# First layer's bias written into PSUM by ScalarE, PSUM's bits set by four early products of zeros, row sums moved to the second step

## The reference

```python
x = ln(x + L0(x, adj));  x = ln(x + L1(x, adj));  x = ln(x + L2(x, adj));  x = ln(x + L3(x, adj))

# L0
y = (adj @ x + x) @ weight + bias
y = y / max(sqrt(sum(y * y, axis=2)), 1e-12)
# L1: five steps of a gated update
m = adj @ h;  av = concat([m, m]);  u3 = h @ u3_w.T + u3_b
z = sigmoid(av @ w3_w.T + w3_b + u3);  r = sigmoid(av @ w4_w.T + w4_b + u3)
h = (1 - z) * h + z * tanh(av @ w5_w.T + w5_b + (r * h) @ u5_w.T + u5_b)
# L2
d = sum(adj + I, axis=-1) ** -0.5;  out = (d * (adj + I) * d.T @ x) @ W.T + b
# L3: a softmax over chosen edge values takes the place of adj, with one weight for the diagonal
```

## Time and profile before

| | |
|---|---|
| median of 3 runs | 779.51 us (778.82 to 779.86) |
| the profiled execution, its own time | 777.98 us |
| its span, first to last instruction | 776.2 us |
| TensorE / VectorE / ScalarE / GpSimd busy | 98% / 80% / 66% / 21% |
| TensorE's granted clock, mean | 0.995 |

### The profile page before, as it was taken

How to read it: one execution, slowest core, us unless ns; L and a number is a source line. 1 busy time by engine, 2 the same in 40 slices (tenths; PEclk the granted TensorE clock), 3 DMA queues, 4 the chain that set the end, 5 groups by cost and what they waited for, 6 DMA issues and landing times.

```text
span 776.2 us, 12043 instructions
## 1 busy us (share of the span) xinstructions
PE 758.7 (98%) x3814; PEld 634.6 (82%) x3814; DVE 623.9 (80%) x1436; ACT 515.9 (66%) x1075; POOL 161.4 (21%) x314
## 2 busy tenths in 40 slices
PE   7999999999999999999999999999999998999996
PEld 6888888888888888888888888888888786788885
DVE  5898898888888887777777777788999898885543
ACT  4698786666667666666666666666677779974344
POOL 1688520000000000000000000000112278653334
PEclk9999999999999999999999999999999999999998
DMA  6200000000030010000000000000000000000112
GB/s 218 98 1 2 1 2 0 1 1 1 0 116 1 1 55 1 1 1 0 1 1 0 0 0 0 0 0 2 1 0 2 1 1 1 2 2 28 55 55 81
DMA packets 8934, 14.24 MB, mean 18 GB/s; under 512 B 2352, under 2 KB 3888, under 8 KB 8496
## 3 DMA queue, kind: packets, MB, share of 16 engines
q1 hardware_dynamic: 8880, 13.58, 5.1%
HBM read 8.33 MB, written 5.24 MB: 17 GB/s over the span
## 4 chain that ended last, share of the span: by engine, by line
PE 85%; DVE 6%; ACT 4%; issue 2%; POOL 1%; DMA 1%; SPq 0%; DVEq 0%; ACTq 0%
PE agg_ps L943 13%; PE agg_ps L945 13%; PE agg_ps L944 13%; PE gate_ps L872 6%; PE gate_ps L874 6%; PE gate_ps L873 6%; PE cand_ps L872 4%; PE cand_ps L874 4%; PE cand_ps L873 4%; PE turn_ps L982 4%; PE gate_ps L879 3%; PE cand_ps L879 3%; ACT res L408 2%; PE turn_ps L986 2%; DVE stats L782 1%
## 5 line engine op out<-in xcount | busy, mean ns | idle before, releaser
L943 PE MATMUL agg_ps<-adj_hi,nat_hi 128*128 128x512 f32 x384 | 152.0, 396 | 0.0
L945 PE MATMUL agg_ps<-adj_hi,nat_lo 128*128 128x512 f32 x384 | 150.1, 391 | 0.0
L944 PE MATMUL agg_ps<-adj_lo,nat_hi 128*128 128x512 f32 x384 | 149.6, 390 | 0.0
L598 POOL TENSOR_SCALAR shift<-mean_var 128x4 f32<-128x4 f32 x64 | 21.8, 341 | 563.4 <-DVE mean_var L786 561.0
L739 DVE TENSOR_TENSOR agg_lo<-agg_ps,agg_hi 128x512 fp32r<-128x512 f32 x80 | 55.2, 690 | 67.6 <-ACT agg_hi L437 67.4
L470 ACT ACTIVATE reset_hi<-gate_r 128x512 fp32r<-128x512 f32 x80 | 50.6, 633 | 81.9 <-DVE gate_r L756 81.9
L945 PEld LDWEIGHTS agg_ps<-adj_hi,nat_lo 128*128 128x128 f32 x384 | 72.1, 188 | 16.2
L944 PEld LDWEIGHTS agg_ps<-adj_lo,nat_hi 128*128 128x128 f32 x384 | 72.2, 188 | 15.6
L454 ACT ACTIVATE gate_r<-gate_ps,bias 128x512 f32<-128x512 f32 x80 | 55.2, 689 | 44.5 <-PE gate_ps L874 44.5
L943 PEld LDWEIGHTS agg_ps<-adj_hi,nat_hi 128*128 128x128 f32 x384 | 72.1, 188 | 15.1
L437 ACT ACTIVATE agg_hi<-agg_ps 128x512 fp32r<-128x512 f32 x80 | 47.8, 597 | 51.1 <-PE agg_ps L945 51.1
(11 more groups left out here) (182 smaller groups left out, 1785.7 us busy)
## 6 DMA issues: line engine op xcount, KB each, us to landing
res<-in_x SPq DMA_DIRECT2D x16, 256.0 KB, 5.7
out<-res SPq DMA_DIRECT2D x16, 256.0 KB, 2.0
rows<-in_adj SPq DMA_DIRECT2D x4, 256.0 KB, 4.0
later<-in_adj SPq DMA_DIRECT2D x1, 1024.0 KB, 6.4
mix_rows<-mix SPq DMA_DIRECT2D x1, 1024.0 KB, 8.0
later<-mix_rows SPq DMA_DIRECT2D x1, 1024.0 KB, 4.8
gate_z<-in_L_gnn_w_w SPq DMA_DIRECT2D x3, 128.0 KB, 4.9
gate_z<-in_L_gnn_u_w SPq DMA_DIRECT2D x2, 64.0 KB, 4.5
```

Of the source, the lines that this page charges most:

```text
L943: pe.matmul(ps, nat_hi[:, b, k, :], m_hi[:, k, :], start=(k == 0), stop=False)
L944: pe.matmul(ps, nat_hi[:, b, k, :], m_lo[:, k, :], start=False, stop=False)
L945: last = pe.matmul(ps, nat_lo[:, b, k, :], m_hi[:, k, :], start=False, stop=(k == T - 1))
```

## The change

The bias is loaded into a third row of `bias_rows`. ScalarE writes it, repeated four times along the columns, into PSUM once per unit, in slot s for unit s, after the squares and ahead of the input split. TensorE's bias product goes, and `layer(u)` waits for `bias_seeded` in its place. As the products that follow must add to what ScalarE wrote, four products of zeros at the very start set the bits of the four banks, and the preparation of the adjacency uses the turn banks and no longer the gate banks. The wait for `rows_read` moves from TensorE to ScalarE. The split of the bias on ScalarE and VectorE goes. The four row sums move from slots 3 to 6 to slots 37 and 38, two in each, and read `later`; `SCALE_AT` moves from 38 to 40, `L2_AT` from 41 to 43, GpSimd's `row_d` to slot 39.

```diff
-SUM_AT = 3
+SUM_AT = VALUE_AT[-1] + 2
-SCALE_AT = VALUE_AT[-1] + 3
+SCALE_AT = SUM_AT + 3
-        bias_parts = sb("bias_parts", [P, D], F32R)
-        bias_rows = sb("bias_rows", [P, 2, D])
-        pick = sb("pick", [P, P], F32R)
+        bias_rows = sb("bias_rows", [P, 3, D])
+        zeros = sb("zeros", [P, P], F32R)
-        prep_ps = agg_ps + gate_ps
+        prep_ps = agg_ps + turn_ps
 # SP
-            sp.dma_start(bias_in, row(b0).to_broadcast([P, D])).then_inc(first_in, 16)
+            sp.dma_start(bias_rows[:, C_L0, :], row(b0).to_broadcast([P, D])).then_inc(first_in, 16)
 # ScalarE, ahead of its slots
-            act.wait_ge(first_in, 32)
-            act.activation(bias_parts[:, :], bias_in, ACT.Copy).then_inc(bias_hi_made, 1)
 # ScalarE, slot s, behind the squares
+                if s < B:
+                    if s == 0:
+                        act.wait_ge(first_in, 32)
+                        act.wait_ge(bits_set, len(layer_ps))
+                    if s >= 4:
+                        act.wait_ge(rows_read, s - 4 + 1)
+                    act.activation(layer_ps[s % 4][:, :].rearrange("p (t d) -> p t d", t=T),
+                                   bias_rows[:, C_L0:C_L0 + 1, :].to_broadcast([P, T, D]), ACT.Copy).then_inc(bias_seeded, 1)
-                k = s - SUM_AT
-                if 0 <= k < T:
-                    act.wait_ge(adj_in[k], 16)
-                    if k:
-                        act.wait_ge(row_sum_made, k)
-                    act.activation(feat[:, 15, :], rows[:, k, :], ACT.Copy, accum_out=row_sum[:, k:k + 1]).then_inc(row_sum_made, 1)
+                for k in range(2 * (s - SUM_AT), 2 * (s - SUM_AT) + 2):
+                    if 0 <= k < T:
+                        act.wait_ge(rows_again, 16)
+                        act.activation(chosen[:, k, :], later[:, k, :], ACT.Copy,
+                                       accum_out=row_sum[:, k:k + 1]).then_inc(row_sum_made, 1)
 # GpSimd
-                if s == SUM_AT + T:
+                if s == SUM_AT + 2:
 # VectorE, ahead of its slots
-            link(dve.memset(pick[:, :].bitcast(F32), 0.0))
-            for row in (0, P // 4):
-                dve.memset(pick[row:row + 1, :].bitcast(F32), 1.0).then_inc(pick_made, 1)
+            dve.memset(zeros[:, :].bitcast(F32), 0.0).then_inc(zeros_made, 1)
-            dve.wait_ge(bias_hi_made, 1)
-            low = slice(P // 4, P // 2)
-            dve.tensor_tensor(bias_parts[low, :], bias_in[low, :], bias_parts[low, :].bitcast(F32),
-                              ALU.subtract).then_inc(bias_made, 1)
 # TensorE, at its start
+            pe.wait_ge(zeros_made, 1)
+            for ps in layer_ps:
+                pe.matmul(ps[:, :].rearrange("p (t d) -> p t d", t=T), zeros[:, :],
+                          zeros[:, :].rearrange("p (o d) -> p o d", o=1).to_broadcast([P, T, D]), start=True,
+                          stop=True).then_inc(bits_set, 1)
 # TensorE, layer(u)
                 if u == 0:
                     pe.wait_ge(first_in, 32)
-                    pe.wait_ge(pick_made, 2)
-                    pe.wait_ge(bias_made, 1)
                 if u < B:
-                    if u >= 4:
-                        pe.wait_ge(rows_read, u - 4 + 1)
-                    pe.matmul(ps[:, :].rearrange("p (t d) -> p t d", t=T), pick[:, :],
-                              bias_parts[:, :].rearrange("p (o d) -> p o d", o=1).to_broadcast([P, T, D]), start=True,
-                              stop=False, skip_group_check=True)
+                    pe.wait_ge(bias_seeded, u + 1)
```

More of the change, by code:

```diff
@@ L222, in graph_layers @@
         owner_b = w_all[:, W_SELF, 0:P // 2].bitcast(BF16)
-        C_L2, C_L3 = range(2)
-        bias_parts = sb("bias_parts", [P, D], F32R)
-        bias_rows = sb("bias_rows", [P, 2, D])
-        pick = sb("pick", [P, P], F32R)
+        C_L0, C_L2, C_L3 = range(3)
+        bias_rows = sb("bias_rows", [P, 3, D])
+        zeros = sb("zeros", [P, P], F32R)
         ident = sb("ident", [P, P])
@@ L257, in graph_layers @@
         RAW_W3, RAW_W4, RAW_W5, RAW_U3, RAW_U5 = 0, 2 * D, 4 * D, 6 * D, 7 * D
-        bias_in = gate_r[:, 0, 0:D]
         raw2 = cand[:, 0, 2 * D:3 * D]
@@ L274, in graph_layers @@
         const_made, consts = sem("const_made"), 6
-        pick_made, bias_hi_made, bias_made = sem("pick_made"), sem("bias_hi_made"), sem("bias_made")
+        zeros_made = sem("zeros_made")
         chain_dve, chain_pool = sem("chain_dve"), sem("chain_pool")
@@ L301, in graph_layers @@
         squared, length_made, shift_made = sem("squared"), sem("length_made"), sem("shift_made")
-        seeded = sem("seeded")
+        seeded, bias_seeded, bits_set = sem("seeded"), sem("bias_seeded"), sem("bits_set")
         statted, aggregated = sem("statted"), sem("aggregated")
```

## The result

The changed kernel takes 775.9 us against 779.1 for the kernel before on the same chip (medians of 16 runs each): a ratio of 0.9964, with a 95% interval of 0.9953 to 0.9975, so 1.9 to 3.7 us. The profiled executions say 777.98 to 775.71, their spans 776.2 to 774.0: 2.3 and 2.2 us. The fastest executions of the changed kernel, at a mean clock of 0.999, take 774.2 to 774.6. Forecast were 776.8 and a gain of 2.7.

A forecast was written before the change was run, and what follows sets the result against it. TensorE, busy 758.7 of 776.2 us, bounds the kernel; ScalarE becomes slowest in the first layer. 2.8 gained there less 0.1 at the start gives 2.7 us: median 779.51 to 776.8, range 775.6 to 778.7.

The forecast's parts named there:

- Sign and size: Whole kernel: faster by 2.7 us, median 779.51 to 776.8 (-0.35%).
- TensorE's 3.6 us: First layer: sixteen bias products at 0.228 us each, 3.6 us that TensorE stops doing.
- The seed's 0.52: ScalarE's write of the bias into PSUM, once per unit, costs 0.52 us, like a plain SBUF to SBUF split.
- rival (1): Bias write on ScalarE is cheap, 0.45 us, or its queue has more slack: gain 3.3 to 3.6 us, 776.1; chance 0.18.
- rival (2): Bias write on ScalarE is dear, each 0.1 us above 0.52 costing ten times that: 778 to 781; chance 0.20.
- ScalarE becomes the bound from slot 7 on: First layer: ScalarE's full slot becomes 4.29 us against TensorE's 4.10; slot 16's copy starts at 78.5, gain there 2.8 us.
- Row sums cost 0 where they go: Slots 37 and 38: two sums each cost 1.2 us of ScalarE time, data covered by 5.4 us; cost 0.
- The ring through rows_read: First layer, rival (3): ScalarE's wait for VectorE's row reads stops its queue; 781.1 and more; chance 0.07.
- The start, 0.1 lost: First slots: bias write ahead of the input split makes VectorE 0.5 us later; the "before" product waits 0.1 us.
- ScalarE's slot taken from starts: First layer: instruction costs read from start to next start, as printed durations are too long; full slot 3.77 + 0.52 = 4.29 us.
- VectorE's stretch passes the shift on, TensorE gives the rest back in waits: After the first layer: VectorE's full stretch moves as a block by 2.8 us; TensorE waits 0.8 us more in slots 17 to 20.
- The distance to the median: Whole kernel: median of the runs lies 1.5 us above the profiled execution, forecast 775.3.

The follow-up runs named there:

- e3: Changed kernel with the first layer's bias left out altogether, no seed and no product; ratio 0.9961 to the kernel before, landmark gain 3.49 us.
- e4: Changed kernel with one more ScalarE copy of the same rows, into SBUF, ahead of each bias write; ratio 1.0042 to the kernel before.
- e6: e5 with the bias of units 7 and 10 by TensorE's old product instead of ScalarE's write; ratio 0.9978 to the kernel before, landmark gain 3.01 us.
- e1: Kernel before with only the row sums moved to slots 37 and 38, bias still a product; ratio 0.9994 to the kernel before.
- e2: Changed kernel with the row sums put back into slots 3 to 6; ratio 0.9982 to the kernel before, landmark gain 1.06 us.
- e5: Changed kernel with ScalarE's bias writes of slots 0 to 3 put behind input split and adjacency copy; ratio 0.9966 to the kernel before.
- e7: Kernel before with only the four early products of zeros added; ratio 1.0000 to the kernel before.

## Why the prediction was right, step by step

- **Sign and size**: right, 775.9 for 776.8, inside the range. By profile the gain is 2.2 us, by landmark 2.0, by ratio 1.9 to 3.7; forecast 2.7. That the medians moved by 3.3, more than forecast, is in part luck: executions of the same mean clock differ by about 2 (at 0.996 the kernel before took 777.5 to 778.2 beside the experiments, the changed one 775.7 to 775.9; at 0.999 776.2 to 776.3 and 774.2 to 774.6). The rest of the 3.3 would be how the executions fell into the clock groups; that is not shown, as the clocks of the sixteen executions of the kernel before aren't known.
- **TensorE's 3.6 us**: right. e3 shows 3.5.
- **The seed's 0.52**: right, in both targets (e4). With it went rival (1), which wanted 0.45 and agg_hi at 77.9, and rival (2), of 0.6 and more.
- **ScalarE becomes the bound from slot 7 on**: right; slots of 4.29, 41.65 us from slot 6 to slot 16 for 41.7, agg_hi at 78.73 for 78.5. TensorE's own slots are 4.10 there, as forecast (its weight products start at 40.50, 44.60, 48.70, 52.80 and 56.90), so it runs ahead of ScalarE. e4 and e6 confirm the bound from both sides.
- **Row sums cost 0 where they go**: right. ScalarE after, slot 37, where the first pair lies between the old state's split and z:

```profile
226.62 0.62 ACT L503 ACTIVATE chosen<-later 128x512 f32<-128x512 f32 x1
...
227.24 0.62 ACT L503 ACTIVATE chosen<-later 128x512 f32<-128x512 f32 x1
...
227.85 0.68 ACT L415 ACTIVATE gate_z<-gate_ps,bias 128x512 f32<-128x512 f32 x1
```

  These are 1.23 us for the 1.2 forecast, while TensorE is busy for 100.00 of the 100 us from 200 on. The load of `later` is issued at 214.54 and lands after 6.3 us, 5.8 before the sums read it; 5.4 were forecast. That their leaving slot 6 is worth something only with the seeds is e1 against e2.
- **The ring through rows_read** (rival 3): refuted. ScalarE had no idle time before any of the sixteen seeds.
- **The start, 0.1 lost**: the mechanism was right (seed, input split, scan, adj_lo, "before" product), the size was not: 0.53 to 0.59. The step went wrong in two ways. It priced the wait of one product only; TensorE's arrival 0.7 us earlier (25.49 for 26.18 before) makes the small product of the following slot wait for VectorE too, which ends there at about the same time as before. And its 0.1 for the first turned out 0.23 by the distance of the slots.
- **ScalarE's slot taken from starts**: this is the term that was missing. It had the starts right and the ends 0.4 us later than these say, after ten slots without a pause (0.04 a slot, so slots of 4.33 by their ends). VectorE's split behind the same ScalarE instruction shows it: it starts at 60.94 and next at 65.27, 4.33 apart.

```profile
60.94 0.69 DVE L632 TENSOR_TENSOR nat_lo<-res,nat_hi 128x512 fp32r<-128x512 f32 x1 [0.32 <-ACT nat_hi L494]
...
65.27 0.69 DVE L632 TENSOR_TENSOR nat_lo<-res,nat_hi 128x512 fp32r<-128x512 f32 x1 [0.32 <-ACT nat_hi L494]
```

  By ends, the full slots 7 to 12 of the changed kernel last 4.33 us, as long as before (4.26 in slot 7, 4.33 in the others): there the products taken off TensorE did not bring ScalarE's results any earlier, they only let TensorE run ahead. The 2.2 us come from elsewhere. By the ends of ScalarE's copies, 0.85 are there at slot 6, and nearly all the rest, 1.35, comes in slots 13 to 15, where TensorE set 4.73, 4.52 and 4.33 before and ScalarE's queue now takes 4.35, 4.08 and 3.80.

  The account at the first agg_hi: before its end was at 81.91. Forecast 2.8; slot 6's copy 0.3 later than forecast (37.08 for 36.79), the longer duration 0.4: 2.1, and 81.91 - 79.73 = 2.2 is what there is.
- **VectorE's stretch passes the shift on, TensorE gives the rest back in waits**: right in kind, but at another product than I named. The wait at the reset product is hardly longer than before (96.12 behind 95.64, 0.25 more than the 0.23 between products; 0.20 more before). TensorE after waits earlier:

```profile
84.95 0.50 PE L876 MATMUL cand_ps<-agg_hi,w_hi 128*128 128x512 f32 x1 [0.66 <-DVE res L705]
```

  TensorE's weight product of the last first-layer unit is 3.1 us earlier than before (78.23 for 81.34), the reset product 2.2, and this wait is most of the 0.9 given back between them; 0.24 more had gone in slot 14, 4.53 long for e3's 4.29. The product needs a bank whose rows VectorE still has to read for the last units of the first layer; in the kernel before the product followed the turns without such a wait. After that, nothing: from the reset product to the end are 677.9 us before and after.
- **The distance to the median**: the profiled execution was taken to lie 1.5 below the median; it lay 0.15 below. The forecast of 775.3 for the profiled execution missed by 0.4, the one for the median by 0.9 the other way.

The growth of the durations is read from traces: the copy stays at 0.60 in e3, where ScalarE waits for TensorE in every slot, and in e6 it comes back to 0.60 where ScalarE has caught up with TensorE. What in the engine makes it grow, no run here shows.

## What to carry to other kernels

When work moves to an engine that then has no idle time, the gain is set by that engine's slot, so add up its queue from the last instruction that still waits, and read the slot from ends or from the consumer's starts, not from the starts alone. Look at the first slots apart: an instruction put ahead of others there delays a chain that is free later on, and placing it last brought 0.6 us here by landmark. And where the receiving engine falls behind by a few per cent only, try leaving one or two of the moved pieces at the old place; that brought 0.4 more by landmark. Neither shows in the timed ratios, whose intervals are wider than these gains.

## What the runs showed of the hardware

- ScalarE writes a 128x512 tile into PSUM at the price of one into SBUF in a full queue: 0.52 us each.
- A product adds onto what ScalarE wrote in PSUM, once an early product of zeros has written the bank and none starts it anew (the changed kernel; no run leaves the products of zeros out, so that they are needed isn't shown); four such products before the data arrives cost nothing (ratio 1.0000).
- In a ScalarE queue without a pause the printed duration of one and the same copy grew from 0.60 to 1.00 us in ten slots. In e6, where ScalarE catches up with TensorE, it was back at 0.60: at the first agg_hi after a pause of 0.18 us, one slot earlier after one of 0.01.
- At a wait of 2.5 us TensorE's granted clock fell to 0.50 (1.2 GHz) in eight of the ten traces and not in the other two (e2, e3), at a cost of 1.2 us, or of 2.4 where it stayed there for nearly 7 us (e5, e6, e7).
- A like fall between 11 and 14 us in e1, e5 and e7 (granted clock 0.50) goes with ScalarE's copy of slot 0 at 15.07 to 15.57, against 13.16 to 13.68 in the other traces.
